# Offsets read back shifted from memory, a batch's mixing three slots later, and new slots for the convolutions

## The reference

```python
# layer 0, on g = _gn(x): pixels mix with pixels
xn = g / max(norm over channels, 1e-8)
s  = relu(xn^T xn) ** 2                       # 1024 x 1024 for each batch
x  = x + (W g + b) s^T

# layer 1, on h = _gn(x)
offset = conv3x3(conv3x3(h, w1, b1), w2, b2)  # 72 channels: 4 groups x 9 taps x (dy, dx)
py = dy + ky + row;  px = dx + kx + column    # each tap samples h bilinearly at (py, px), zero outside
val = bilinear samples, for each group, tap and pixel
x  = x + relu(sum over channels and taps of wd * val)
```

## Time and profile before

| | us |
|---|---|
| median of three runs | 515.77 (515.76 to 515.89) |
| the profiled execution's own time | 515.51 |
| its span, first to last instruction | 513.80 |
| TensorE busy | 428.8 (83%) |
| VectorE busy | 344.2 (67%) |
| ScalarE busy | 224.7 (44%) |
| GpSimd busy | 140.7 (27%) |
| mean granted TensorE clock, as a share of full speed | 0.947 |

### The profile page before, as it was taken

The page is one execution under the profiler, slowest core; times in us unless marked ns, Lnnn a source line. Parts: engine busy times, 40 slices in busy tenths (PEclk is TensorE's granted clock), DMA queues, the critical chain, the costliest instruction groups (busy, mean ns, idle before and its releaser), DMA issues.

```text
span 513.8 us, 9711 instructions
## 1 busy us (share of the span) xinstructions
PE 428.8 (83%) x3881; PEld 304.9 (59%) x3881; DVE 344.2 (67%) x582; ACT 224.7 (44%) x404; POOL 140.7 (27%) x179
## 2 busy tenths in 40 slices
PE   2899799967998988779998987878798976888886
PEld 2666465734665656557665654657565654666665
DVE  4619996499988983954657992745979538199400
ACT  2046133224565453414655453314765333178640
POOL 3266441343872102102763101101210101031100
PEclk9999799997999989989999989879998987999999
DMA  3400000201111113011101112011210121023211
GB/s 122 169 1 1 1 1 1 46 1 21 22 22 22 22 22 65 6 40 31 33 15 27 22 22 56 23 33 41 43 24 20 25 64 33 20 52 64 42 33 33
DMA packets 22187, 17.23 MB, mean 34 GB/s; under 512 B 1981, under 2 KB 20669, under 8 KB 22141
## 3 DMA queue, kind: packets, MB, share of 16 engines
q1 hardware_dynamic: 21884, 16.07, 12.9%
q10 hardware_dynamic: 256, 0.52, 0.7%
HBM read 3.74 MB, written 3.28 MB: 14 GB/s over the span
## 4 chain that ended last, share of the span: by engine, by line
PE 58%; DVE 24%; ACT 7%; issue 5%; DMA 3%; ACTq 2%; SPq 1%; DVEq 0%
PE psB L719 13%; PE psB L506 12%; PE psA L586 8%; DVE wpix L1342 6%; PE psV L695 5%; PE psA L506 5%; PE psT L672 5%; ACT wcell L897 3%; DVE tent L1323 2%; PE psT L662 2%; DMA hwin<-hwin 2%; PE psA L562 2%; DVE tent L1317 2%; DVE combo L1135 2%; ACT val L910 2%
## 5 line engine op out<-in xcount | busy, mean ns | idle before, releaser
L897 ACT ACTIVATE wcell<-psT 128x512 f32<-128x512 f32 (+1 forms) x160 | 83.4, 552 | 82.3 <-PE psT L672 73.6
L1342 DVE TENSOR_TENSOR wpix<-tent 128x512 f32<-128x512 f32 (+1 forms) x160 | 107.1, 720 | 16.0 <-PE psT L672 15.0
L672 PE MATMUL psT<-ident,wpix 128*128 128x128 f32 x576 | 86.5, 283 | 14.5 <-ACT wcell L897 13.5
L672 PEld LDWEIGHTS psT<-ident,wpix 128*128 128x128 f32 x576 | 66.9, 144 | 38.8 <-issue 28.7
L447 POOL COPY strips<-hring 128x256 f32<-128x256 f32 x64 | 43.3, 702 | 155.8 <-PE psT L662 155.8
L424 POOL TENSOR_TENSOR sim<-rel 128x512 f32<-128x512 f32 x48 | 60.3, 1276 | 62.4 <-ACT rel L858 62.4
L719 PE MATMUL psB<-val,wd_sb 128*128 128x256 f32 x288 | 73.5, 412 | 3.6 <-issue 3.6
L719 PEld LDWEIGHTS psB<-val,wd_sb 128*128 128x128 f32 x288 | 57.7, 206 | 15.6 <-issue 7.2
L695 PE MATMUL psV<-wcell,hwin 64*32 64x144 f32 x2048 | 48.5, 300 | 13.3 <-DMA hwin<-hwin 13.3
L910 ACT ACTIVATE val<-psV 128x576 f32<-128x576 f32 x64 | 44.0, 688 | 34.2 <-PE psV L695 22.7
L506 PE MATMUL psB<-g_p 128*128 128x512 f32 x144 | 44.6, 448 | 6.7 <-DVE g_p L1075 6.7
(11 more groups left out here) (166 smaller groups left out, 498.0 us busy)
## 6 DMA issues: line engine op xcount, KB each, us to landing
hwin<-hwin SPq DMA_DIRECT2D x64, 128.0 KB, 2.5
out<-yout SPq DMA_DIRECT2D x16, 128.0 KB, 1.8
x_all<-x SPq DMA_DIRECT2D x1, 1536.0 KB, 8.9
off_scr<-sim SPq DMA_DIRECT2D x4, 288.0 KB
combo<-sim SPq DMA_DIRECT2D x20, 32.0 KB
val<-w SPq DMA_DIRECT2D x1, 576.0 KB
wd_sb<-wd SPq DMA_DIRECT2D x1, 576.0 KB
x_all<-x SPq DMA_DIRECT2D x1, 512.0 KB, 3.5
```

Of the source, the lines that this page charges most:

```text
L672: last = pe.transpose(bank[:, at:at + P], wpix[:, t % 2, k, 2 * h:2 * h + 2, :].rearrange("p g q -> p (g q)"), ident[:, :])
L897: act.activation(wcell[:, t % 2, taps[0]:taps[-1] + 1, :, :].rearrange("q k h p -> q (k h p)"), bank[:, 0:len(taps) * G // 2 * P], ACT.Cop ...
L1342: dve.tensor_tensor(w, ty, tx, ALU.mult).then_inc(s["weights_done"], 1)
```

## The change

- Offsets: SP copies the patches of tile 6 first. It then saves the whole ring with its ends (72 rows of 1090) to memory, waits for that, and reads the nine taps back with three copies; each covers one row of taps, and its source pattern steps back by one element from tap to tap. ScalarE issues none.
- `diagonal` of batch 2 gets a tile of its own, over `orelu` and `yout`, and no longer waits for batch 0's extremes; these are taken at slot 12 of batch 0 in place of slot 65 of the lead. `diagonal` stands in front of `low`.
- The mixing of batch 2 runs three slots later (`LAG`).
- Batch 1's mean, variance and normalisation stand at slots 1, 2 and 5 of batch 0 (`OPENING`), and batch 2's scores wait for its standard deviation. For later batches the steps from the mean to the normalisation stand at 23, 23, 24 and 25.
- Row combinations and convolutions stand a slot later, and the weights of tiles 5, 6 and 7 at other slots.

```diff
+        ends_out = sb("ends_out", [P, 2, HALF])
+        orelu, yout = (ends_out[:, i, :].rearrange("p (j n) -> p j n", j=2) for i in range(2))
...
-                    shift=57, turn={59: (0, 1), 61: (2, 3)}, extremes=65)
-        STEADY = dict(mean=23, dev=24, var=25, norm=28, combine=(29, 42), high=(30, 43), conv=(35, 48), wrap=54,
-                      shift=56, turn={60: (0, 1), 61: (2, 3)}, extremes=66)
+                    turn={59: (0, 1), 61: (2, 3)}, extremes=None)
+        STEADY = dict(mean=23, dev=23, var=24, norm=25, combine=(29, 43), high=(30, 44), conv=(36, 48), wrap=54,
+                      turn={60: (0, 1), 61: (2, 3)}, extremes=66)
+        OPENING = dict(STEADY, mean=1, dev=1, var=2, norm=5)
+        LAG = 3
...
-        PREP_THIRD = {57: ("normalise", "square"), 58: ("norms", "invert"), 59: ("bias",), 64: ("high",), 65: ("low",),
-                      66: ("diagonal",)}
+        PREP_THIRD = {57: ("normalise", "square"), 58: ("norms", "invert"), 59: ("bias",), 64: ("high",), 65: ("diagonal", "low")}
...
         W_AT = {2: (0, 1, 3, 5, 6), 3: (9, 10, 12, 14, 15), 4: (18, 19, 21, 23, 24),
-                5: (31, 32, 33, 35, 36), 6: (37, 38, 40, 44, 45), 7: (47, 48, 50, 51, 52)}
+                5: (36, 36, 37, 37, 38), 6: (48, 48, 49, 49, 50), 7: (51, 51, 54, 55, 56)}
...
+        def shifted(b, y):
+            at = (b * NOFF + 3 * y * 2 * G) * HELIX + TURN - shift(3 * y)
+            return bass.AP(off_dram, at, [[2 * G * HELIX - 1, 3], [HELIX, 2 * G], [1, NPIX]])
...
                 sp.wait_ge(s["off_wrapped"], 2 * b + 2)
-                shift_taps(sp, range(BY_SYNC))
-                sp.dma_start(off_scr[bass.ds(b, 1), :, :].rearrange("b n q -> n (b q)"),
-                             off_ring[:, TURN:TURN + NPIX]).then_inc(s["off_saved"], 16)
+                sp.dma_start(off_scr[b, :, :], off_ring).then_inc(s["off_saved"], 16)
+                sp.wait_ge(s["off_saved"], 16 * (b + 1))
+                for y in range(3):
+                    sp.dma_start(off_ch[3 * 2 * G * y:3 * 2 * G * (y + 1), :], shifted(b, y)).then_inc(s["off_shifted"], 16)
...
-                for t in range(ROWT - 2):
+                for t in range(ROWT - 1):
                     cross(b, t)
                 if b + 1 < B:
                     shift_offsets(b + 1)
-                cross(b, ROWT - 2)
                 store(b, 0)
...
+                    if b == 2:
+                        pe.wait_ge(s["sd_done"], 2)
                     pe.wait_ge(s["g_lo_done"], b + 1)
...
-                            mix_front(b + 2, n)
+                            mix_front(b + 2, n - LAG * (b == 0))
...
-                            conv_front(nxt, n, STEADY, prep)
+                            conv_front(nxt, n, STEADY if b else OPENING, prep)
...
-                if n == at["shift"]:
-                    act.wait_ge(s["off_wrapped"], 2 * b + 2)
-                    shift_taps(act, range(BY_SYNC, K))
...
-                    if b >= 2:
+                    if b >= 3:
                         dve.wait_ge(s["extremes_done"], 2 * (b - 1))
...
+                        if b == 0 and n == LEAD_EXTREMES:
+                            find_extremes(0)
```

More of the change, by code:

```diff
@@ L212, in mix_deform_kernel @@
                             lent[:, NPIX:2 * NPIX])
+        out_diag = ends_out[:, :, :].rearrange("p j n -> p (j n)").rearrange("p (i q) -> p i q", q=P)
+        third_tiles = Mixing(inv2_all[:, :], gsq, gxT, out_diag, sim, psB, psA, scratch[:, :])
         def tiles(b):
-            return lent_tiles if b == 1 else own_tiles
+            return {1: lent_tiles, 2: third_tiles}.get(b, own_tiles)
         s = {n: sem(n) for n in (
@@ L232, in mix_deform_kernel @@
         out_sems = [s["out_first"], s["out_second"]]
-        off_scr = nc.dram_tensor("off_scr", [B, NOFF, NPIX], F32, kind="Internal").ap()
+        off_dram = nc.dram_tensor("off_scr", [B, NOFF, HELIX], F32, kind="Internal")
+        off_scr = off_dram.ap()
         block = ctx.enter_context(nc.Block())
@@ L273, in mix_deform_kernel @@
         ZEROED = 5
-        SHIFTS = 16 * K
-        BY_SYNC = 5
+        SHIFTS = 16 * 3
         CONV_INPUTS = 4 + K
@@ L365, in _ @@
                     sp.wait_ge(s["g_offT"], b + 1)
-                    sp.dma_start(off_raw, off_scr[bass.ds(b, 1), :, :].rearrange("b n q -> n (b q)"))\
+                    sp.dma_start(off_raw, off_scr[bass.ds(b, 1), :, TURN:TURN + NPIX].rearrange("b n q -> n (b q)"))\
                         .then_inc(s["g_off"], 16)
@@ L469, in batch_steps @@
                         n = K * t + k
-                        if b + 2 < B and n in SCORE:
-                            square(b + 2, SCORE.index(n))
+                        step = n - LAG * (b == 0)
+                        if b + 2 < B and step in SCORE:
+                            square(b + 2, SCORE.index(step))
                         if nxt is not None and n == STEADY["wrap"]:
@@ L523, in group_mean @@
             def group_mean(b, col):
-                if b > 0 and col == 0:
+                if b > 1 and col == 0:
                     pe.wait_ge(s["orelu_done"], 4 * (b - 1) - 1 + ORELU0)
@@ L954, in batch_steps @@
                         if nxt is not None:
-                            conv_front(nxt, n, STEADY)
+                            conv_front(nxt, n, STEADY if b else OPENING)
                 take_samples(b, ROWT - 1, 0)
@@ L1282, in conv_front, with find_extremes @@
                 if n == at["extremes"]:
-                    dve.wait_ge(s["off_shifted"], SHIFTS * (b + 1))
-                    for i, op in enumerate((ALU.max, ALU.min)):
-                        dve.tensor_reduce(extremes[:, i, b:b + 1], off_ch, AX.X, op)\
-                            .then_inc(s["extremes_done"], 1)
+                    find_extremes(b)
+            def find_extremes(b):
+                dve.wait_ge(s["off_shifted"], SHIFTS * (b + 1))
+                for i, op in enumerate((ALU.max, ALU.min)):
+                    dve.tensor_reduce(extremes[:, i, b:b + 1], off_ch, AX.X, op)\
+                        .then_inc(s["extremes_done"], 1)
             def place_in_order(b, j):
```

4 lines of the change are left out of this document (1 added, 3 removed).

## The result

The changed kernel takes 530.86 us (median of 4 runs, 530.15 to 531.63); the kernel before took 515.83 in the same comparison (4 runs). The ratio is 1.0291, interval 1.0273 to 1.0309: 2.9% slower. 536 was forecast, with 516 to 550 as the range. The profiled execution took 531.1, its span is 529.4; so +15.6 of span against +20.1 forecast. Kernels are compared by executions that agree with each other; one execution of the kernel of experiment 8 took 814.18 us and is left out of its median.

What follows compares the result with a forecast made beforehand. TensorE was taken as the engine to follow: full in the third batch's mixing, elsewhere waiting in handoffs and at the offsets' turn. 9.4 − 9.1 + 16.8 + 3.0 = +20.1 on 515.51 us gave 535.6, say 536; range 516 to 550.

Steps and rivals of the forecast that it cites:

- The opening: First batch's opening: the third batch's scores wait for VectorE's variance step and start 10.6 us later; +9.4 us in all.
- The offsets' way: Save and three reads through memory before the turn of the offsets, 11.3 us from the save's issue; +16.8 us.
- Three engines a read: Offset reads: source's outermost count of 3 puts each read on three DMA engines, the same three for all.
- the row: Offset reads: a 4 KB row costs 0.29 us, 24 rows 6.9 us; bounds of a row 0.24 and 0.5.
- Its start: Offset reads: a first byte comes 1.2 us after an issue.
- the save: Offsets' ring saved to memory before the reads: landing taken at 3.2 us, bounds 1.8 and 3.6.
- the lead's 2.1: Turn before the first batch: offsets there at 103.5 against TensorE at the turn at 101.4, +2.1 us.
- The convolutions: Three convolution stretches: new slots remove TensorE waits before, inside and between the convolutions; -9.1 us, bounds 0 and -20.1.
- 0.85 + 1.5 in each: Gain per batch: 0.85 us from a wait inside the first convolution, 1.5 us between the two convolutions.
- the 1.05 and 0.35: Ahead of the first convolution: the first batch gains 1.05 us, the second 0.35.
- The third batch's 0.65: Ahead of the first convolution: the third batch gains 0.65 us.
- The clock: Output convolution's six matmuls between the two turns run at lower clock, 1.0 us in each batch; +3.0, bounds 0 and 4.3.

Runs made afterwards that it cites:

- experiment 8: Experiment 7's kernel with the first convolution at slot 35 in place of 36: 511.59 us, ratio 0.9925.
- experiment 5: Changed kernel with VectorE's `spread(1)` moved between the third batch's diagonal and g_p, the lag kept: 522.82 us, ratio 1.0145.
- experiment 6: Changed kernel without the three-slot lag, the early mean and the scores' wait for `sd_done`: 522.35 us, ratio 1.0131.
- experiment 1: Changed kernel with the three reads' source flat, outermost count 24 in place of 3, one-pixel shift left out: 521.29 us, ratio 1.0126.
- experiment 2: Changed kernel with nine reads of 8 rows, shift kept, in place of three of 24: 524.81 us, ratio 1.0198.
- experiment 7: Changed kernel with the offsets' nine direct copies as before and no lag, leaving the tables alone: 515.13 us, ratio 1.0002.
- experiment 10: Changed kernel with VectorE waiting for GpSimd's wrap copies before tile 7's last three products: 532.74 us, ratio 1.0351.
- after: The changed kernel itself, against the kernel before: 530.86 us, ratio 1.0291.
- experiment 3: Kernel before with only the offsets' way through memory put in (save, wait, three reads): 531.41 us, ratio 1.0325.
- best: Experiment 8's kernel with VectorE waiting for the wrap copies before tile 7's last three products: 511.03 us, ratio 0.9915.

## Why the prediction was nearly right

**The opening: right.** +9.4 forecast, +9.4 from turn to mixed sums. Tile 1's tents and products took 4.8 us (5.3 forecast), and from `varp` to the scores it was 1.5, as taken. Undone, with the diagonal still ahead of g_p, it gives back 7.5 to 8.2 (experiments 5, 6).

**The offsets' way: right mechanism, size too large.** Forecast +16.8 in four places, measured 0.3 + 3.9 + 2.2 + 2.6 = +9.0. Three engines a read was right: the share was 0.17 to 0.18, and experiments 1 and 2, whose only common change is the outermost count, both turn the delay down. The term mis-sized is the row, 0.29 us forecast and 0.20 measured: 24 rows in 4.8 us and not 6.9. Its start took 1.6, not 1.2; the save 3.1, as taken (3.2). 9.8 us in place of 11.3 makes 1.5 at each of four places, 6.0 of the 7.8 that are missing. The rest is mostly the second and third batch's save, which left 0.7 us earlier than I had it: SP's patch copies came 1.2 us after the output row and not 2.6, and what the save waited for last was GpSimd's wrap copy, over at 3.05. And 0.4 of the lead's 2.1 was a misreading: the earlier trace rows has TensorE at the turn at 101.80, not 101.4. The 0.29 came from a row that has 1.2 of start taken off a landing of 3.5; of the two bounds beside it, 0.24 would have been nearer (5.8 us for 24 rows) and 0.5 further off. In the lead the delay nearly vanished: the turn waited 0.17 us for the reads.

The Trainium skill's rule that a DMA uses the largest number of engines up to 16 that divides the slowest dimension of both patterns ("DMA: Bandwidth & Descriptors", "Why a DMA increments its semaphore by 16 and not by 1") holds for a count of 3: the trace agrees with 0.17 and 0.18. For 24 it gives 12 engines; experiment 1 shows 0.63 while its reads start and end, which neither contradicts nor proves 12; nor does the 0.38 of experiment 2 prove 8.

**The convolutions: right inside, wrong ahead of them.** Forecast -9.1, measured -6.8 (the 1.3 of the clock, below, taken out): from the first convolution's first matmul to the second's -2.0 - 3.0 - 2.8 (forecast 0.85 + 1.5 in each, 7.1 in all), ahead of the first +0.2, behind the second's first matmul +0.8. The terms that failed are the 1.05 and 0.35 ahead of the first convolution (measured +0.2 and 0). I shortened VectorE's chain and did not ask what stood before the convolution on TensorE once it was at slot 36: tile 4's turn, waiting for ScalarE. Experiment 8 shows it, since one slot brought 0.7 of it back in each of the two batches where I could read it. The third batch's 0.65 stays open: from tile 7's sample to the first convolution experiments 5, 6, 7 and 10, with the same slot 36, take 38.3 to 38.4 us against 39.25 before, but at a granted clock of 0.95 to 0.96 over that stretch against 0.91. For the loss behind the second convolution I had no term either.

**The clock: right in size, not in place.** +3.0 forecast from turn to sample, +3.7 measured. Another 1.3 came ahead of the third batch's first convolution (40.57 us against 39.25 from the sample), where the granted clock is 0.77 and not 0.86; that is why the table shows only -1.4 in the third batch's stretch and not -2.7. Experiments 5, 6 and 10, with the same way and tables there, have 0.87 and 38.3 us, so this part is no fixed price of the change. The six matmuls between the turns take 2.86 us in the third batch (2.5 to 2.9 forecast). Cutting the wait from 7.8 to 4.4 us (experiment 1) gave nothing of it back in the second batch up to the sample: turn to sample is 15.0 us there, 15.15 in after. Behind the sample 1.5 us came back, at a clock of 0.88.

**Sum.** Lead -1.8, batches' way -6.0, convolutions +2.3, clock +0.7 and +1.3, the stretches for which I had no term -1.0 (start-up among them): -4.5, from 535.6 to 531.1. That the sum came so near is in part luck: the way was 7.8 us too dear, and the convolutions and the clock, 4.3 too cheap together, made up for half of it.

**What the sum hid.** Each part was priced against the kernel before, and the parts aren't independent. Without the lag, the four combinations are: neither 1, tables 1.0002, way 1.0325, both 1.0131. The tables are worth nothing on the direct way and 10 us on the way through memory. They do two things to the offsets: they delay the wrap copy, and they bring tile 6's patch copies from 2.6 to 1.2 us behind the output row. On the direct way only the delay counts, and the turns come 2.0, 0.8 and 1.4 later (experiment 7). On the way through memory the save stands behind both, so it leaves 3.1 us after the output row and not 4.0, and between experiments 3 and 6 the turns of the second and third batch come 1.4 and 1.3 earlier. Some 2 us more lie behind the second batch's tile 7, where experiment 3 lost them. So my -9.1 was near the truth only beside the way through memory, and for partly other reasons; on the direct way the opposite sign of the turn would have made it nearly nothing.

## What to carry to other kernels

Before giving a copy a third dimension to save issues, look at its outermost count: three long reads over an outermost count of 3 were slower than nine short ones over 8, here 6.8 us against 4.8 from first issue to use. When a step is brought forward on the consumer, follow every engine up to it: the three-slot lag cost 8 us since VectorE had a whole tile of other work in front of a 0.22 us operation. And where a table moves work from one gap to another, look at the engine that shares the new gap.

## What the runs showed of the hardware

A 72 x 33 copy on GpSimd takes 0.21 us alone and 1.55 beside VectorE's 128 x 512 products, in every kernel that has them there. It is as if it waited for them to end: 323.66 + 1.55 is 325.21, and they end at 325.14. Holding them back (`best`) brings 0.21 back, as in the kernel before:

```profile
313.80 0.21 POOL L453 COPY sim<-sim 72x33 f32<-72x33 f32 x1 [13.07 <-DVE sim L1164]
```

With one such product beside it, in the first batch, it takes 0.61.

The Trainium skill says that VectorE and GpSimd share a pair of ports as an exclusive lock, which a VectorE operation with two inputs in SBUF takes for its whole length against a GpSimd operation that reads SBUF ("SBUF — State Buffer", "SBUF: two separate sides"). By this rule, the trace agrees with 1.55, 0.61 and 0.21, and adds that the copy got in at none of the gaps between three products in a row. I didn't weigh it in the prediction, though the change puts products there.

An issue of the three-dimensional read costs SP 0.78 us (2.34 for three); the flat one 0.38 (1.15 for three) and an 8-row one 0.33 (3.00 for nine).

The scatter of these kernels goes with TensorE's clock: twelve runs of `best` lie between 506.73 us at a mean granted clock of 0.956 and 513.62 at 0.94. With waits of 2.4 to 3.8 us before the fourth batch's norms, they and the logits run at the lower level for some or all of their length. After the 0.52 us of the kernel before they did not, but in `memory_alone` they did behind the same 0.52 us (2.27 and 3.76 us), so this wait alone does not decide it.
